# One transformer layer on one core: storing the split gate and up weights in the first pass and loading them in the three others

## The reference

```
x      = fwht(x * SU_ug) / SCALE
x_up   = x @ W_up.T   * (Wscale_ug[:2048] * SCALE)
x_gate = x @ W_gate.T * (Wscale_ug[2048:] * SCALE)
x = silu(x_gate) * x_up
x = fwht(x * SU_dp) / SCALE
x = x @ W_down.T * (Wscale_dp * SCALE)
```

## Time and profile before

| | |
|---|---|
| median of 3 runs | 2294.93 us (2291.66 to 2295.72) |
| the profiled execution | 2294.09 us, its span 2292.3 us |
| PE busy in the span | 2252.4 us, 98% |
| DVE, ACT, POOL busy | 80%, 56%, 49% |
| granted TensorE clock | 0.997 of full speed |
| all DMAs | 252.87 MB, mean 110 GB/s |
| third stage | from 1312 us to the end |

### The profile page before, as it was taken

The page is one execution under the profiler, slowest core; times in us unless marked ns, Lnnn a source line. Parts: engine busy times, 40 slices in busy tenths (PEclk is TensorE's granted clock), DMA queues, the critical chain, the costliest instruction groups (busy, mean ns, idle before and its releaser), DMA issues.

```text
span 2292.3 us, 32686 instructions
## 1 busy us (share of the span) xinstructions
PE 2252.4 (98%) x10226; PEld 1823.2 (80%) x10226; DVE 1830.6 (80%) x2482; ACT 1273.6 (56%) x2285; POOL 1126.9 (49%) x1004
## 2 busy tenths in 40 slices
PE   9899999999999999999999999999999999999998
PEld 7677878787878786788888778888888888888887
DVE  7877787868686868788888897787888788868877
ACT  7666666667676767243444555454445545554543
POOL 5666776767676767455544733322342133303311
PEclk9999999999999999999999999999999999999999
DMA  4021211102020115777678532223223322222313
GB/s 157 35 70 38 70 47 55 64 37 72 30 73 32 69 65 190 256 258 255 238 260 269 172 129 74 106 88 110 88 88 101 111 88 95 94 79 86 104 60 102
DMA packets 132710, 252.87 MB, mean 110 GB/s; under 512 B 44576, under 2 KB 45344, under 8 KB 122880
## 3 DMA queue, kind: packets, MB, share of 16 engines
q1 hardware_dynamic: 132608, 251.60, 32.7%
HBM read 188.11 MB, written 63.44 MB: 110 GB/s over the span
## 4 chain that ended last, share of the span: by engine, by line
PE 71%; issue 11%; POOL 9%; DVE 6%; ACT 2%; DMA 1%; SPq 0%; POOLq 0%; ACTq 0%; DVEq 0%
PE pj L626 16%; PE pj L709 11%; PE pnum L709 6%; PE pj L723 5%; PE psc L709 5%; PE pst L709 4%; PE psc L723 4%; PE pj L636 3%; PE pnum L723 3%; PE psc L657 3%; PE pnum L677 3%; PE pnum L680 3%; PE pst L723 2%; POOL fb L1416 1%; POOL fa L1415 1%
## 5 line engine op out<-in xcount | busy, mean ns | idle before, releaser
L1445 POOL TENSOR_TENSOR wcs<-wcr 128x256 f32<-128x256 f32 x64 | 67.6, 1056 | 514.4 <-DVE wcl L1187 505.4
L1482 POOL TENSOR_TENSOR tb<-tb,sinb 128x512 f32<-128x512 f32 x160 | 224.1, 1401 | 79.7 <-ACT tb L1007 79.4
L1485 POOL TENSOR_TENSOR Ql<-tb,Qh 128x512 fp32r<-128x512 f32 x128 | 171.2, 1340 | 65.6 <-ACT Qh L1016 65.6
L547 PE MATMUL pj<-woh,oh 128*128 128x512 f32 x512 | 202.1, 395 | 0.0
L626 PE MATMUL pj<-xah,wqh 128*128 128x512 f32 x500 | 198.2, 396 | 3.2 <-DVE Kf L1322 2.4
L547 PE MATMUL pj<-woh,ol 128*128 128x512 f32 x512 | 200.1, 391 | 0.0
L547 PE MATMUL pj<-wol,oh 128*128 128x512 f32 x512 | 199.8, 390 | 0.0
L626 PE MATMUL pj<-xah,wql 128*128 128x512 f32 x500 | 194.9, 390 | 0.0
L626 PE MATMUL pj<-xal,wqh 128*128 128x512 f32 x500 | 194.8, 390 | 0.0
L1310 DVE TENSOR_TENSOR pj<-pj,cosb 128x512 f32<-128x512 f32 x156 | 108.3, 695 | 69.9 <-ACT tb L1007 69.8
L1492 POOL TENSOR_SCALAR_AFFINE_SELECT Ah<-Ah 128x512 fp32r<-128x512 f32 x128 | 101.8, 795 | 112.7 <-DVE Al L1351 112.2
(11 more groups left out here) (287 smaller groups left out, 7115.3 us busy)
## 6 DMA issues: line engine op xcount, KB each, us to landing
num_scratch<-no SPq DMA_DIRECT2D x128, 256.0 KB, 2.4
nt<-num_scratch SPq DMA_DIRECT2D x32, 1024.0 KB, 5.4
rb<-rden_scratch SPq DMA_DIRECT2D x32, 1024.0 KB, 6.7
wdr<-wd_scratch SPq DMA_DIRECT2D x128, 256.0 KB, 3.2
wcr<-in_wg SPq DMA_DIRECT2D x64, 256.0 KB, 2.8
wcr<-in_wu SPq DMA_DIRECT2D x64, 256.0 KB, 3.1
xst<-in_xT SPq DMA_DIRECT2D x34, 256.0 KB, 3.8
xr<-in_x SPq DMA_DIRECT2D x32, 256.0 KB, 5.6
```

The source lines that it names most:

```text
L547: last = nc.tensor.matmul(py[s][:, :], a[s][:, h, :], b[:, h, :], start=(h == 0 and i == 0), stop=(h == H - 1 and i == 2))
L1482: nc.gpsimd.tensor_tensor(tb[c][:, :], tb[c][:, :], sinb[:, :], ALU.mult).then_inc(sin_done, 1)
L1485: nc.gpsimd.tensor_tensor(Ql[g % 2][:, c, :], (tb[c] if c else Kf)[:, :], f32(Qh[g % 2][:, c, :]), ALU.subtract).then_inc(lo_done, 1)
```

## The change

A new scratch tensor in HBM, `parts_d`, holds `wch` and `wcl` of all 16 blocks. In pass 0 SP stores both after `weights_lo` of the block is done (`store_parts`, two DMAs of 0.92 MB). In passes 1 to 3 SP loads both straight into the buffers that PE reads (`load_parts`), and `load_weights`, `weight_sums`, `weights_hi` and `weights_lo` do nothing for n >= 16. PE waits for the loads in place of DVE's lower parts. In pass 0 ACT waits, before it writes into a buffer of `wch`, that the stores of the block two back have landed.

```
+        parts_out, parts_in = [sem(f"parts_out{i}") for i in range(2)], [sem(f"parts_in{i}") for i in range(2)]
...
-                pe.wait_ge(w_lo, 3 * n + 1)
+                if n < FB:
+                    pe.wait_ge(w_lo, 3 * n + 1)
+                else:
+                    pe.wait_ge(parts_in[n % 2], 32 * ((n - FB) // 2 + 1))
...
             def weights_hi(n, i):
-                if n < NS2 * FB:
+                if n < FB:
...
                     if n >= 2:
                         act.wait_ge(product_done, (n - 1) * NP)
+                        act.wait_ge(parts_out[n % 2], 32 * (n // 2))
...
             def weights_lo(n, i):
-                if n < NS2 * FB:
+                if n < FB:
...
             def weight_sums(n):
-                if n < NS2 * FB:
+                if n < FB:
...
+            def store_parts(n):
+                if n < FB:
+                    sp.wait_ge(w_lo, 3 * n + 3)
+                    for i, a in enumerate((wh, wl)):
+                        sp.dma_start(parts_d[n, i], f32(wide(a[n % 2][:]))).then_inc(parts_out[n % 2], 16)
+
+            def load_parts(n):
+                if FB <= n < NS2 * FB:
+                    if n == FB:
+                        for i in range(2):
+                            sp.wait_ge(parts_out[i], 16 * FB)
+                    sp.wait_ge(product_done, (n - 1) * NP)
+                    for i, a in enumerate((wh, wl)):
+                        sp.dma_start(f32(wide(a[n % 2][:])), parts_d[n % FB, i]).then_inc(parts_in[n % 2], 16)
+
             def load_weights(n):
-                if n < NS2 * FB:
+                if n < FB:
...
+                    load_parts(m * FB + f + 1)
                     load_weights(m * FB + f + 3)
+                    if m == 0 and f == 0:
+                        store_parts(0)
+                    store_parts(m * FB + f + 1)
                     load_down(m * 2 * FB + f + WDS)
```

More of the change, by code:

```diff
@@ L214, with phases @@
 NS2 = T // TWO
-def phases(nc, xT, wq, wk, wv, cosT, sinT, x, wo, su, consts, wd, sd, wsd, wg, wu, wsg, wsu, num_d, den_d, rden_d, x1_d, x2_d, wd_d, out):
+def phases(nc, xT, wq, wk, wv, cosT, sinT, x, wo, su, consts, wd, sd, wsd, wg, wu, wsg, wsu, num_d, den_d, rden_d, x1_d, x2_d, wd_d, parts_d, out):
     ctx = ExitStack()
@@ L751, in gate_up @@
                 product(m, f, 1, b, True)
-                pe.wait_ge(w_lo, 3 * n + 3)
+                if n < FB:
+                    pe.wait_ge(w_lo, 3 * n + 3)
                 pe.wait_ge(chain_out, 3 * n + 1)
@@ L1817 @@
     wd_d = scratch("wd_scratch", [P, FB, D])
+    parts_d = scratch("parts_scratch", [FB, 2, P, NP * (DC // 2) * P])
     phases(nc, a["xT"], a["wq"], a["wk"], a["wv"], a["cosT"], a["sinT"], a["x"], a["wo"], a["su"], a["consts"], a["wd"], a["sd"],
-           a["wsd"], a["wg"], a["wu"], a["wsg"], a["wsu"], num_d, den_d, rden_d, x1_d, x2_d, wd_d, out)
+           a["wsd"], a["wg"], a["wu"], a["wsg"], a["wsu"], num_d, den_d, rden_d, x1_d, x2_d, wd_d, parts_d, out)
     r = run_bass_kernel_spmd(nc, [feed], core_ids=[0])
```

## The result

The changed kernel takes 2306.15 us in the median of 6 runs (2304.24 to 2311.12), the kernel before 2294.12 in 6 runs. The ratio is 1.0056 (1.0045 to 1.0067): slower by 0.56%, where 2307 had been forecast. The profiled execution has a span of 2304.3 us, 12.0 more than before.

What follows compares the result with a forecast made beforehand. PE was taken to bound the third stage, with the removed work beside it. 7.0 + 1.7 + 3.9 + 3.05 - 2.6 = 13.05 us on 2294.09 gave 2307.1, stated as 2307; 8-in-10 range 2300 to 2318 us.

Steps and rivals of the forecast that it cites:

- The stage is bound by PE and the removed work is free: Third stage: removed ACT, DVE and POOL work costs PE nothing but two kinds of waits; -2.6 us, between 0 and -2.9.
- the entries of the down steps: Passes 0 to 2: without POOL's sums beside it `hl` takes 0.69 us, not 1.18; -1.5 us in all.
- the 1.1 of step 8: Step 8 of passes 1 and 2: DVE no longer late without the lower parts, -0.56 x 2 = -1.1 us.
- Block 0's stores land behind the activations: Step 1 of pass 0: stores queue behind `xcr` loads, land at 1343.9; PE idles 7.5 us, net +7.0 us.
- The clock: Pass 0, after PE's 7.5 us idle: about 3.4 us at half clock, +1.7 us, bounds 0 and 3.4.
- Steps 8: f = 8, three times: parts queue behind the `x1r` load, late by 1.3 us each, +3.9 us.
- Steps 0 of passes 1 and 2: f = 0: parts queue behind four `xcr` loads, late by 0.7 and 2.35 us, +3.05 us.
- Steps 3 to 7, 9 and 10 are early: Passes 1 to 3: parts issued after the `out` store land at 10.3 us, early by 1.7; cost 0.
- The rate: Parts' transfers: 413 GB/s, 4.4 us a block in pass 0; 380 GB/s, 4.8 us in passes 1 to 3.
- The rivals at 256 and at 358 GB/s: Parts move at 256 GB/s, 2328 us, chance 0.06; 358 GB/s as hard limit, 2309.4 us, inside the forecast's 0.83.
- The half clock after a late load: Passes 1 to 3, rival: half clock returns after each of five late loads, +8.5, 2315.6 us; inside the forecast's 0.83.

Runs made afterwards that it cites:

- experiment 1: The kernel before, with weights' sums, upper and lower parts neither formed nor loaded from n = 16 on: 2291.72 us, ratio 0.9989.
- experiment 2: The kernel before plus only pass 0's stores and ACT's wait for their landing, nothing loaded: 2304.13 us, ratio 1.0043.
- experiment 3: The changed kernel with block 0's stores issued before the last x1 rows are stored, not behind block 3's raw weights: 2297.33 us, ratio 1.0015.
- experiment 4: The changed kernel with the next pass's activation loads at f = 1 in place of f = 0 in passes 1 and 2: 2303.38 us, ratio 1.0034.
- experiment 5: The changed kernel with the residual rows' loads behind the parts' loads at f = 8 and 13, not ahead: 2303.07 us, ratio 1.0034.
- experiment 10: The changed kernel with one more unused 0.92 MB load per block in passes 1 to 3, ahead of the two: 2333.21 us, ratio 1.0167.
- experiment 7: The changed kernel with 33 unused matmuls filling PE's idle time in step 1 of pass 0: 2307.64 us, ratio 1.0062.
- experiment 8: The changed kernel with 28 unused matmuls filling PE's idle time in step 1 of pass 0: 2307.53 us, ratio 1.0050.

## Why the prediction was right

- **The stage is bound by PE and the removed work is free.** Right: experiment 1 gives 2.9 us at most. The forecast had 2.6. The changed kernel's profile shows 2.2 at the entries of the down steps (1.5 forecast) and, once the loads are in time, the 1.1 of step 8. The reason given for the entries holds: from 1545 us on `hl` (L1274, now L1280) takes 0.68 us in the mean where it took 1.16.
- **Block 0's stores land behind the activations.** Right in place and size: ACT's wait 8.91 us against 8.8, PE's idle time 7.53 against 7.5. Experiments 2 and 3 put the loss there from two sides. That it agrees to the tenth is luck: in the profiles of experiments 2, 4, 5 and 10, whose code is the same up to there, PE idled 7.2 to 8.4 us.
- **The clock.** The mechanism is in the profile, the term was too small: 5.8 us of work at half the clock, 2.9 us, where 1.7 had been put in with 3.4 as the upper end. Experiments 7 and 8 give back 2.7 of it. The half clock lasts longer after 7.5 us of idling than after the 3 us of the earlier trace rows.
- **Steps 8.** The place is right, the term of 3.9 less 1.1 was too large: net 1.6 us. SP got to its `out` store 2.3 us into step 8 of pass 2, as forecast with the faster tail of DVE. The late parts cost 0.8, 1.3 and 0.6 us in the three passes, where 1.3 had been put in for each; PE idled 0.3 to 1.1 us.
- **Steps 0 of passes 1 and 2.** 3.6 us against 3.05.
- **Steps 3 to 7, 9 and 10 are early.** Right. The lower parts land 8.8 to 11.4 us into the step where 10.3 was forecast and 12.05 needed. In experiment 10 some of these steps are over the edge.
- **The rate** of 410 to 430 GB/s holds for rows of 7168 bytes, in stores and loads. In the changed kernel the stretch from 1340.2 to 1344.4 us moved stores alone, at 423 GB/s; in the loads the lower parts land 2.18 us behind the upper parts in the median, which is 0.92 MB at 421 GB/s. The rivals at 256 and at 358 GB/s are out: the Trainium skill (DMA: Bandwidth & Descriptors, Specifications) names about 358 GB/s as a core's limit to HBM, and these two rates are above it.

The sum was 13.05 us, the steps add up to 12.9: the errors of +1.2 (clock), -1.2 (steps 8), +0.6 (steps 0) and -0.7 (entries) nearly cancel. That is luck, and the number was closer than its parts. The half clock after a late load, which was left out of the sum, did not come in the changed kernel's profile, whose longest such wait is 1.75 us. It did come in that of experiment 5 and five times in that of experiment 10, behind waits of 2.0 us and more.

## What to carry to other kernels

Work on engines beside the bound one is worth what the bound engine waits for it, here 2.9 us for 400 us of busy time; read that before trading it for transfers. When transfers are added to a queue, cost their place and not only their size: what is ahead of them, and who stands behind the instruction that waits for them. Three moves in SP's order turned a kernel that was slower by 0.56% into one that is faster by 0.14%, with not a byte less.

## What the runs showed of the hardware

- 7168-byte rows: in the changed kernel two loads of 0.92 MB land 4.8 and 6.7 us after their issues in the median, the second 2.18 us behind the first (421 GB/s), and stores alone were moved at 423 GB/s.
- Behind some 2.6 MB in the same queue two such stores landed 9.9 and 11.4 us after their issues, and 4.3 and 6.6 us after them in experiment 3, where they were issued early.
- PE kept its distance of 0.227 us beside 263 GB/s of DMAs, most of them loads into the buffers that it reads from (experiment 10).
- Half the clock came after idle times of PE of 7.5 us (changed kernel), 3.0 and 2.0 (experiment 5), but not after each of this length: before the change, 2.55 us passed without it. After 7.5 us it stayed for 5.8 us of work and cost 2.7 to 2.9.
